# A two-layer expert network behind a graph sum: expert queues of 44-byte records, rows gathered by token in the expert stage

## The reference, cut

```python
# x: (50000, 256) f32; src, dst, edge_weight: 25000 edges, sorted by dst
x = x + _L0_gnn_ref(_layernorm(x), src, dst, edge_weight)
    # f16: rows H[dst] * weight, summed into row src
x = x + _L0_ffn_ref(_layernorm(x)[None], gate_w, gate_b, w1, b1, w2, b2)[0]

def _L0_ffn_ref(h, ...):                      # E = 8 experts, D = 256, F = 1024
    probs = softmax(h @ gate_w + gate_b)
    idx = argmax(probs); prb = probs[idx]
    pos = place of the token in the queue of its expert
    kept = pos < C                            # C = ceil(1.25 * T / E)
    hmid = relu(h @ w1[idx] + b1[idx])
    y = (hmid @ w2[idx] + b2[idx]) * prb * kept
    return nan_to_num(y, nan=0, posinf=1e4, neginf=-1e4)
```

## Time and profile before

| what | value |
|---|---|
| median of 3 runs | 3663.58 us (3653.1 to 3665.04) |
| span of the profiled execution, first to last instruction | 3533.8 us |
| PE busy | 2919.1 us (83%) |
| DVE busy | 2291.9 us (65%) |
| POOL busy | 1796.0 us (51%) |
| ACT busy | 1564.2 us (44%) |
| HBM read and written | 184.33 and 195.85 MB |

### The profile page before, as it was taken

One profiled execution on the slowest core, in us unless ns is written; L12 is line 12 of the kernel. 1 busy time (PEld: TensorE's weight loads), 2 busy tenths in 40 slices (PEclk: granted clock), 3 DMA queues, 4 the chain that ended last, 5 costly groups with the idle time before them and its releaser, 6 DMA issues.

```text
span 3533.8 us, 60004 instructions
## 1 busy us (share of the span) xinstructions
PE 2919.1 (83%) x18982; PEld 2664.8 (75%) x18983; DVE 2291.9 (65%) x5804; ACT 1564.2 (44%) x2603; POOL 1796.0 (51%) x1195
## 2 busy tenths in 40 slices
PE   4544434078888876999999999999999999999998
PEld 3433434078888875988989988888988989998987
DVE  6655455077777764676676676676676676667666
ACT  2322222045555543554454555454555444454453
POOL 4788887647777773334343333434333433334332
PEclk8766666555555557999999999999999999999999
DMA  9544444399999963111111111111111121111110
GB/s 344 135 86 76 90 76 87 29 290 302 306 307 292 281 201 111 49 52 62 55 54 50 49 45 51 62 53 59 49 44 50 42 68 41 49 55 32 49 46 26
DMA packets 303467, 371.32 MB, mean 105 GB/s; under 512 B 35431, under 2 KB 263812, under 8 KB 300080
## 3 DMA queue, kind: packets, MB, share of 16 engines
q1 hardware_dynamic: 221504, 199.21, 19.2%
q0 software_dynamic: 78304, 145.23, 15.4%
q10 hardware_dynamic: 3600, 26.22, 1.8%
HBM read 184.33 MB, written 195.85 MB: 108 GB/s over the span
## 4 chain that ended last, share of the span: by engine, by line
PE 55%; DVE 3%; issue 2%; DVEq 1%; DMA 0%; SPq 0%; POOL 0%; ACT 0%; POOLq 0%; ACTq 0%
PE u_Y L1125 29%; PE u_H L1114 24%; PE u_T L1099 2%; DVE y L1058 1%; DVE yo L1077 1%; DVE yo L1074 0%; DVE y L1063 0%; DVE hn L1029 0%; DVE low L1068 0%; DVE hlo L1047 0%; DVE yo L1072 0%; DMA u_pay<-slots 0%; DMA slots<-blank 0%; DVEq L882 0%; DVEq L881 0%
## 5 line engine op out<-in xcount | busy, mean ns | idle before, releaser
L967 POOL DMA_INDIRECT out_x<-yo,u_token x360 | 712.3, 1979 | 1330.5 <-DVE yo L1079 1243.7
L1125 PE MATMUL u_Y<-whi,hhi 128*128 128x256 f32 x2880 | 816.0, 283 | 2.2 <-DVE hlo L1047 2.2
L999 ACT ACTIVATE hm<-u_H,b1e 128x512 f32<-128x512 f32 x720 | 496.3, 689 | 712.3 <-PE u_H L1114 684.0
L1125 PE MATMUL u_Y<-wlo,hhi 128*128 128x256 f32 x2880 | 807.2, 280 | 0.0
L1125 PE MATMUL u_Y<-whi,hlo 128*128 128x256 f32 x2880 | 806.2, 280 | 0.0
L1114 PE MATMUL u_H<-xhi,whi 128*128 128x512 f32 x1440 | 570.8, 396 | 3.1 <-DVE xlo L1036 2.5
L1114 PE MATMUL u_H<-xlo,whi 128*128 128x512 f32 x1440 | 570.3, 396 | 0.0
L1114 PE MATMUL u_H<-xhi,wlo 128*128 128x512 f32 x1440 | 570.0, 396 | 0.0
L1125 PEld LDWEIGHTS u_Y<-whi,hhi 128*128 128x128 f32 x2880 | 545.1, 189 | 2.4 <-DVE hlo L1047 2.4
L1125 PEld LDWEIGHTS u_Y<-wlo,hhi 128*128 128x128 f32 x2880 | 545.0, 189 | 0.0
L1125 PEld LDWEIGHTS u_Y<-whi,hlo 128*128 128x128 f32 x2880 | 544.3, 189 | 0.0
(11 more groups left out here) (127 smaller groups left out, 3757.4 us busy)
## 6 DMA issues: line engine op xcount, KB each, us to landing
xt<-in_x SPq DMA_DIRECT2D x49, 1024.0 KB
out_x<-pay SPq DMA_DIRECT2D x49, 1024.0 KB, 6.0
u_pay<-slots SPq DMA_DIRECT2D x91, 534.0 KB, 3.9
agg<-zeros ACTq DMA_DIRECT2D x25, 1024.0 KB, 10.9
at<-agg SPq DMA_DIRECT2D x49, 512.0 KB
raw<-in_L_ffn_w POOLq DMA_DIRECT2D x14, 1024.0 KB, 6.9
src_row<-in_src SPq DMA_DIRECT2D x25, 512.0 KB
slots<-pay,slot_i POOLq DMA_INDIRECT x392
```

The costliest lines, as they stand in the source:

```text
L967: pool.indirect_dma_start(out=out[:, :], out_offset=bass.IndirectOffsetOnAxis(ap=token[:, s:s + 1], axis=0), in_=yo[:, s, :], in_offset=No ...
L999: act.activation(hm[:, f, :], ps_H[:, f % 2, :], ACT.Relu, bias=b1e[:, f:f + 1])\
L1125: last = pe.matmul(ps_Y[:, s, 0:D], a[:, f, cols], w2_at(w, buf, f), start=(f == 0 and j == 0), stop=(f == KF - 1 and j == 2))
```

## The change

Queues hold records of 11 numbers (44 bytes: mean, reciprocal deviation, token, 8 logits). Routing keeps the rows in `x1` and the records in `rec`, stores `x1` to `out` as before and scatters `rec` alone. Loads and the store now give a partition 8 tokens that lie side by side in memory, so the rank needs another triangle `upto` and 8 + 7 + 8 = 23 matmuls in place of 9. The first expert's weight split moves from ahead of the routing loop to behind it. In the expert stage SyncE loads 512 records, GpSimd gathers the 512 rows from `out` by token (4 indirect DMAs for a unit, two units ahead) into one buffer `x1`; ScalarE copies it to one of two `keep` halves (`hold`), which the tail's last addition reads; VectorE copies the record to `own`.

```diff
-MEAN, RSTD, TOKEN, LOGIT = 256, 257, 258, 259
+MEAN, RSTD, TOKEN, LOGIT = 0, 1, 2, 3
@@ route_tokens
-                sp.dma_start(xt[:, r % 2], x[bass.ds(b, STEP), :].rearrange("(g p) d -> p g d", p=P))\
+                sp.dma_start(xt[:, r % 2], x[bass.ds(b, STEP), :].rearrange("(p g) d -> p g d", g=G))\
...
-                        in_=pay[:, r, g, :], in_offset=None, bounds_check=E * QUEUE - 1, oob_is_err=False,
+                        in_=rec[:, r, g, :], in_offset=None, bounds_check=E * QUEUE - 1, oob_is_err=False,
...
-                pe.matmul(ranks[:, 0:G, :], before[:], hot[:, q], start=True, stop=False, skip_group_check=True)
                 for g in range(G):
-                    last = pe.matmul(ranks[:, g + 1:G + 1, :], ones[:],
-                                     hot[:, q, g, :].unsqueeze(1).broadcast_to([P, G - g, E]),
+                    pe.matmul(ranks[:, 0:g + 1, :], before[:], hot[:, q, g, :].unsqueeze(1).broadcast_to([P, g + 1, E]),
+                              start=(g == 0), stop=False, skip_group_check=True)
+                for g in range(G - 1):
+                    pe.matmul(ranks[:, g + 1:G, :], upto[:],
+                              hot[:, q, g, :].unsqueeze(1).broadcast_to([P, G - 1 - g, E]),
+                              start=False, stop=False, skip_group_check=True)
+                for g in range(G):
+                    last = pe.matmul(ranks[:, G, :], ones[:], hot[:, q, g, :],
                                      start=False, stop=(g == G - 1), skip_group_check=True)
...
-                v.tensor_tensor(pay[:, r, :, 0:D], xt[:, q], at[:, q], ALU.add).then_inc(x1_ready, 1)
+                v.tensor_tensor(x1[:, r], xt[:, q], at[:, q], ALU.add).then_inc(x1_ready, 1)
@@ run_experts, SyncE
-                    sp.wait_ge(y_ready, u + (1 - RING + SEED["y_ready"]))
+                    sp.wait_ge(hn_ready, u + SEED["hn_ready"])
                     sp.nop(nofuse=True)
                     load(u, (u * UNIT + at).with_bounds(min_val=0, max_val=E * QUEUE - UNIT))
@@ GpSimd
+            def gather(u):
+                pool.wait_ge(rec_loaded, 16 * (u + 1))
+                pool.nop(nofuse=True)
+                pool.wait_ge(kept, u + SEED["kept"])
+                pool.nop(nofuse=True)
+                for s in range(SUB):
+                    pool.indirect_dma_start(
+                        out=x1[:, s, :], out_offset=None, in_=out[:, :],
+                        in_offset=bass.IndirectOffsetOnAxis(ap=rec[:, s, TOKEN:TOKEN + 1].bitcast(I32), axis=0),
+                        bounds_check=N - 1, oob_is_err=False,
+                    ).then_inc(gathered, 16)
...
                 with pool.Fori(begin, end) as u:
+                    gather(u + LEAD)
                     pool.wait_ge(y_ready, u + 1 + SEED["y_ready"])
@@ ScalarE
+            def hold(u):
+
+                act.wait_ge(gathered, 16 * SUB * (u + 1))
+                if not isinstance(u, int):
+                    act.wait_ge(y_ready, u - 1 + SEED["y_ready"])
+                    act.nop(nofuse=True)
+                act.activation(keep[:, u % 2], x1[:], ACT.Copy).then_inc(kept, 1)
...
-                    act.activation(ex[:], pay[:, u % RING, :, LOGIT:LOGIT + E], ACT.Exp).then_inc(ex_ready, 1)
+                    act.activation(ex[:], own[:, u % 2, :, LOGIT:LOGIT + E], ACT.Exp).then_inc(ex_ready, 1)
+                    hold(u + 1)
                     for f in range(KF):
                         act.wait_ge(first_done, KF * u + (f + 1))
@@ VectorE
-                v.wait_ge(pay_loaded, 16 * (u + 1))
-                v.tensor_copy(scales[:], pay[:, u % RING, :, MEAN:RSTD + 1]).then_inc(scales_ready, 1)
-                v.wait_ge(scales_ready, u + 1)
+                v.wait_ge(gathered, 16 * SUB * (u + 1))
+                v.tensor_copy(own[:, u % 2], rec[:])
...
-                    v.tensor_tensor(yo[:], yo[:], pay[:, u % RING, :, 0:D], ALU.add).then_inc(y_ready, 1)
+                    v.tensor_tensor(yo[:], yo[:], keep[:, u % 2], ALU.add).then_inc(y_ready, 1)
```

More of the change, by code:

```diff
@@ L494, in store @@
                 sp.wait_ge(x1_ready, RING * i + r + 1)
-                sp.dma_start(out[bass.ds(b, STEP), :].rearrange("(g p) d -> p g d", p=P), pay[:, r, :, 0:D])\
+                sp.dma_start(out[bass.ds(b, STEP), :].rearrange("(p g) d -> p g d", g=G), x1[:, r])\
                     .then_inc(out_written[r], 16)
@@ L564, in body @@
                     for g in range(k * G // BANKS, (k + 1) * G // BANKS):
-                        last = act.activation(h[:, q, g, :], pay[:, r, g, 0:D], ACT.Identity,
-                                              bias=shift[:, q, g:g + 1], scale=pay[:, r, g, RSTD:RSTD + 1])
+                        last = act.activation(h[:, q, g, :], x1[:, r, g, :], ACT.Identity,
+                                              bias=shift[:, q, g:g + 1], scale=rec[:, r, g, RSTD:RSTD + 1])
                     last.then_inc(h_ready, 1)
@@ L625, in _ @@
         def _(v):
-            v.wait_ge(pool_set, 5)
-            raw, whi, wlo = t["raw"], t["whi"], t["wlo"]
-            v.tensor_copy(whi[:, 0, :], raw[:]).then_inc(split, 1)
-            v.wait_ge(split, 1)
-            v.tensor_tensor(wlo[:, 0, :], raw[:], whi[:, 0, :].bitcast(F32), ALU.subtract)
+            v.wait_ge(pool_set, 7)
             v.tensor_copy(token[:], token_i[:])
@@ L661, in statistics @@
                 for g in range(G):
-                    last = v.bn_stats(stats[:, g, :], pay[:, r, g, 0:D])
+                    last = v.bn_stats(stats[:, g, :], x1[:, r, g, :])
                 last.then_inc(step, n.inc())
@@ L699, in choice @@
                 v.wait_ge(step_b, n.now())
-                less = pay[:, r, :, LOGIT:LOGIT + E]
+                less = rec[:, r, :, LOGIT:LOGIT + E]
                 v.tensor_tensor(less, lg[:], top[:].unsqueeze(2).broadcast_to([P, G, E]), ALU.subtract)\
@@ L757, in _ @@
             slot(n, 0, Count(LAST * PER_B + CHOICE))
+            raw, whi, wlo = t["raw"], t["whi"], t["wlo"]
+            v.tensor_copy(whi[:, 0, :], raw[:]).then_inc(split, 1)
             n = Count(S * PER_A + SET)
@@ L784, in _ @@
             v.tensor_copy(first_blank[:], filled[:]).then_inc(step, n.inc())
+            v.wait_ge(split, 1)
+            v.tensor_tensor(wlo[:, 0, :], raw[:], whi[:, 0, :].bitcast(F32), ALU.subtract)
 def run_experts(nc, ctx, t):
@@ L819, in run_experts @@
     b2e = sb("b2e", [P, D], F32)
-    pay = sb("u_pay", [P, RING, SUB, W], F32)
+    rec = sb("u_rec", [P, SUB, W], F32)
+    own = sb("own_rec", [P, 2, SUB, W], F32)
+    x1 = sb("u_x1", [P, SUB, D], F32)
+    keep = sb("keep", [P, 2, SUB, D], F32)
     blank = sb("blank", [P, SUB, W], F32)
-    scales = sb("scales", [P, SUB, 2], F32)
     token = sb("u_token", [P, SUB], I32)
@@ L846, in run_experts @@
     blanked = sem("blanked")
+    x1_clear = sem("x1_clear")
     b1_turned = sem("b1_turned")
@@ L868, in run_experts @@
     y_ready = sem("y_ready")
-    scales_ready = sem("scales_ready")
+    kept = sem("u_kept")
     step = sem("u_step")
-    SEED = dict(y_clear=1, prob_ready=1, relu_done=2, hid_ready=KF, y_read=1, y_ready=RING,
+    LEAD = 2
+    SEED = dict(y_clear=1, hn_ready=1, kept=1, prob_ready=1, relu_done=2, hid_ready=KF, y_read=1, y_ready=RING,
                 split=2)
@@ L905, in load @@
             def load(u, row):
-                sp.dma_start(pay[:, u % RING, :, :], slots[bass.ds(row, UNIT), :].rearrange("(s p) w -> p s w", p=P))\
-                    .then_inc(pay_loaded, 16)
+                sp.dma_start(rec[:], slots[bass.ds(row, UNIT), :].rearrange("(p s) w -> p s w", s=SUB))\
+                    .then_inc(rec_loaded, 16)
             def expert(e, buf, begin, end):
@@ L925, in _ @@
             units = sp.value_load(first_unit[0:1, E:E + 1], min_val=E, max_val=E * UMAX)
-            sp.wait_ge(y_ready, units + (1 - RING + SEED["y_ready"]))
-            sp.nop(nofuse=True)
-            load(units, 0)
-            sp.wait_ge(pay_loaded, 16 * (units + 1))
-            sp.nop(nofuse=True)
+            for extra in range(LEAD):
+                sp.wait_ge(hn_ready, units + (extra + SEED["hn_ready"]))
+                sp.nop(nofuse=True)
+                load(units + extra, 0)
+                sp.wait_ge(rec_loaded, 16 * (units + (extra + 1)))
+                sp.nop(nofuse=True)
         @block.gpsimd
@@ L949, in _ @@
             pool.sem_inc(split, SEED["split"])
-            pool.wait_ge(pay_loaded, 16)
-            pool.nop(nofuse=True)
+            pool.memset(x1[:], 0.0).then_inc(x1_clear, 1)
+            pool.wait_ge(x1_clear, 1)
+            def gather(u):
[9 more added lines that the diff above has]
+                    ).then_inc(gathered, 16)
+            gather(0)
+            gather(1)
             load_weights(1)
@@ L974, in _ @@
             experts(pool, expert)
+            units = pool.value_load(first_unit[0:1, E:E + 1], min_val=E, max_val=E * UMAX)
+            pool.wait_ge(gathered, 16 * SUB * (units + LEAD))
```

(4 more changed lines are left out.)

41 lines of the change are left out of this document (24 added, 17 removed).

## The result

The changed kernel takes 4583.45 us (median of 4 runs, 4580.49 to 4594.58) against 3660.99 us for the kernel before beside it: a ratio of 1.2535, 95% interval 1.251 to 1.256, or +922 us. Forecast were 4540 us and +876.

The account below looks back on a forecast made before the run. TensorE was taken to bound the expert stage (23.27 us a unit), GpSimd's scatter preparation the routing (12.0 a step). 908 - 35 + 0 + 3 = 876 us on 3663.6 gave 4540 us, range 4420 to 4690.

Parts of the forecast that it names:

- The bound and the wait: Expert stage: ScalarE's copy waits for y_ready ahead of the relus, so TensorE stands 8.1 us a unit, 89 times.
- One of the signs: Expected in the profile after: ScalarE's hold copy waits some 7 us on VectorE's last addition in nearly every unit.
- The clock: Expert stage: TensorE's clock falls to 0.50 in each gap, costing 2.1 us a unit, from bounds 1.2 and 2.6.
- Rival 1: Expert stage: the wait bites but the clock holds, 89 x 8.1 = 721 us, 4353 in all; chance 5%.
- Changes of expert: Expert stage, seven switches: 4 us lost in place of 9 each, -35 us, bounds -64 and +50.
- Routing: Routing stage: GpSimd's scatter stays at 0.97 us and the step at 12.0, so 0 us, range -35 to +10.
- Start: Start of the experts: two small transfers replace two big ones, four gathers with their landing are added, +3 us.
- Rival 2: Expert stage: hold waits for late gathers, 89 us per microsecond past 42.4; with 2 us, 4718; chance 10%.
- The frame: Whole kernel: the run median 3663.58 us lies 129.8 above the profiled span of 3533.8, kept as it is.
- the plain periods: Expert stage: each unit costs 10.2 us more, period 33.5 in place of 23.27, 89 x 10.2 = 908 us.

Follow-up runs that it names:

- the extra matmuls: The changed kernel with 64 extra matmuls on TensorE between blocks 1 and 2 of each first layer, overwritten before use: 4231.4 us, ratio 1.1979.
- the kernel with four halves: The changed kernel with four `keep` halves in place of two, the copy still ahead of the relus: 4001.8 us, ratio 1.0936.
- the two edits together: The changed kernel with ScalarE's copy behind the relus, the gather ahead of the weight split, and an unused 16-byte tile: 3832.1 us, ratio 1.047.

## Why the prediction was right, point by point

**The bound and the wait.** Right in mechanism and size. The copy waits for the addition of the unit before, 89 times; block 2 was put at 10.9 us into the first layer, and it starts at 10.8; TensorE stands 7.84 ahead of it, in the unit shown and in the median. Moving the copy takes it away, and putting the wait into the kernel before brings 8.7 us a unit. One of the signs was put wrongly: the copy was to wait "some 7 us" and waits 17.09. ScalarE has nothing to do from the exponentials on, and the profile counts its wait from there; TensorE loses only the part behind its block 1.

**The clock.** Mechanism right, term low: 2.1 forecast, 2.5 measured with the clock held up. It came from the bounds 1.2 and 2.6. Rival 1 (the clock holds) is what the extra matmuls make by force, 199 us below the changed kernel; by itself it did not happen, for the slow stretch stands behind the gap in all 89 units.

**What the sum lacked.** 0.16 us a unit, 14 us, in the second layer. I had costed the move of the tiles at nothing, without a row on it.

**Changes of expert.** Put at 7 x -5 = -35 with a bound of -64; measured -59.8. Only six of the seven cost more than 1 us before: the last change brings no split. And of the 4 us that I left at each nothing is left. The split falls on the `hlo` subtractions as said; the chain of waits at such a change in the changed kernel:

```profile
1845.21 9.50 DVE hlo L1092
1854.76 4.54 PE u_Y L1170 x36
```

But the unit that it lengthens by 2.1 to 2.8 us is followed by two that are 0.5 to 1.2 shorter, so the bound from below was the nearer.

**Routing.** Put at 0 between -35 and +10. On A it is -14.5: the long instruction did not go, it became shorter (3.02 to 2.39 in the two shown), and GpSimd's pauses did too. DMA fell from nine tenths to five or six, and the step hardly moved, as forecast. On B the last scatter of the changed kernel starts at 1450.5, and that of the kernel before with its tiles moved at 1444.0, so there it lost 6.5.

**Start.** +3 forecast, +4.9 measured on A.

**Rival 2, late gathers.** Not in the changed kernel: in the unit shown the gathers have landed by about 2534, and the copy that needs them comes a period after 2518.06, at 2552. Its arithmetic was right to ask, though. With the slot free they are what comes next, since the slack that the forecast gave them was the gap's own.

**The frame.** The 129.8 us were kept as time outside the span. They are not. As they were added to both sides, the error cancelled.

In all: 908 - 35 + 0 + 3 = 876 forecast; 963.9 - 59.8 - 14.5 + 4.9 + 1.8 = 896.3 on A. On B the same split, against the kernel before with all its tiles moved, is 966.5 - 51.8 + 6.5 + 6.0 + 1.8 = 929, where the medians of the runs give 922. That the total came within 46 us owes something to errors that cancel: the plain periods were put 56 us too low, and the changes of expert 25 us too high on A and 17 on B.

## What to carry to other kernels

Smaller transfers gave next to nothing here, since the engine that prepares them took 0.97 to 0.98 us for one at any size tried; look at the median of the issuing instruction against the bytes before spending anything on bytes. A step that waits for a slot belongs behind the work that others wait for in the same engine's order: the same copy cost 867 us ahead of the relus and next to nothing behind them. And when a wait is taken away, cost the next one from the same timeline; here freeing the slot instead of moving the copy left 342 of 922 us, most of them to gathers that had been hidden.

## What the runs showed of the hardware that I had not expected

- Where the tiles lie in memory is worth up to 0.68 us in 22.56 to TensorE: the two layers together take 21.88 where the distance between weights and activations is 64 bytes past a multiple of 128, and 22.56 where it is 32. That made 53 us of this kernel for a tile of 16 bytes. The clock was at 1.0 in all of them. With equal addresses a second layer can still take either of two times, 10.98 or 11.39.
- GpSimd's indirect transfer of 128 rows takes 0.97 to 0.98 us whether a row has 44, 556 or 1068 bytes, and one issued during VectorE's addition ends 0.85 us after the addition. It looks the same under the `hlo` subtractions: in the kernel with four halves eight of them in a row end at 1903.05, and the scatter that takes 4.81 ends 0.87 later; three in a row end at 1923.52, and the one of 1.79 ends 0.85 later.
- After gaps of 7.84 us the slow clock lasted 5.7 us of work in the median unit, and 3.0 at the least; after gaps of 6.88 it lasted 3.3 and 5.5 in turn.
- Chips differ in how late VectorE and ScalarE start on what TensorE has finished. On A the routing step is 12.0 us for the kernel before; on B it is (1444.0 + 1 - 750.0)/49 = 14.2, with GpSimd idle for 3.3 us between its groups in place of 0.4. All five traces from B have waits above 0.5 us whose releaser the profile can't name ("remote"), in the edge and routing stages of all and in the expert stage of one, and none of the nine from A has any. The kernel before with its tiles moved, routing:

```profile
999.78 1.95 PE L614 MATMUL ps_T<-ident,h 128*128 128x128 f32 x8
...
1002.41 0.97 POOL L534 DMA_INDIRECT slots<-pay,slot_i  x1 [0.31 <-issue]
1003.57 0.22 DVE L695 TENSOR_TENSOR lg<-ps_L,gb 128x64 f32<-128x64 f32 x1 [5.59 <-remote]
...
1005.04 0.60 ACT L561 ACTIVATE hT<-ps_T 128x512 f32<-128x512 f32 x1 [4.87 <-remote]
```

VectorE starts 0.19 us after the last of eight scatters ends, and ScalarE 3.3 us after the transposes that it copies. It is the picture of the two edits together, where both start shortly after GpSimd's last gather. What delays them was only observed, not tested.
